# Scores of all 16 heads in one unit: four row strips and four PSUM banks at once, in place of two units of two strips

## The reference, cut to what matters

```python
# "gqa" (layer 0): 16 query heads, 4 key heads, width 32
scores = jnp.einsum('btkgd,bskd->bkgts', qg, k) * scale
scores = scores + mask[None, None, None]
p = jax.nn.softmax(scores, axis=-1)
out = jnp.einsum('bkgts,bskd->btkgd', p, v).reshape(B, T, C)
return out @ wo.T + bo
# "decay" (layer 1, self): no softmax
scores = jnp.einsum('bhid,bhjd->bhij', qb, kb) * intra_decay[None]
# "causal" (layer 1, cross): 16 heads, width 32
scores = jnp.einsum('bhqd,bhkd->bhqk', qh, kh) * inv_sqrt_d
scores = jnp.where(causal, scores, jnp.finfo(scores.dtype).min)
attn = jax.nn.softmax(scores, axis=-1)
```

## Time and profile before

| | |
|---|---|
| median of 3 runs | 2109.41 us (2105.24 to 2112.19) |
| the profiled execution | 2104.9 us, its span 2104.9 us |
| TensorE matmul busy | 1932.6 us, 92% |
| TensorE weight loads busy | 1575.4 us, 75% (they overlap the matmuls) |
| VectorE busy | 1044.6 us, 50% |
| ScalarE busy | 711.8 us, 34% |
| GpSimd busy | 386.6 us, 18% |
| mean granted TensorE clock | 0.969 |

### The profile page before, as it was taken

How to read it: one execution, slowest core, us unless ns; L and a number is a source line. 1 busy time by engine, 2 the same in 40 slices (tenths; PEclk the granted TensorE clock), 3 DMA queues, 4 the chain that set the end, 5 groups by cost and what they waited for, 6 DMA issues and landing times. The chain is left out here.

```text
span 2104.9 us, 32789 instructions
## 1 busy us (share of the span) xinstructions
PE 1932.6 (92%) x12124; PEld 1575.4 (75%) x12124; DVE 1044.6 (50%) x1836; ACT 711.8 (34%) x2275; POOL 386.6 (18%) x339
## 2 busy tenths in 40 slices
PE   8999888999999979999899999899979996999991
PEld 6777677788888757877678877677758874899990
DVE  5676753455555455333455556676755232222224
ACT  4555634344444422212221112444632211233332
POOL 2110100000000056000021100000104222644335
PEclk9999999999999989999999999999999998999995
DMA  7211051000000021000290001000015100644257
GB/s 236 59 42 42 1 193 47 1 1 1 1 1 1 1 106 60 0 0 0 92 388 6 1 31 41 1 1 1 2 46 185 66 0 0 240 136 154 80 112 204
DMA packets 73376, 135.89 MB, mean 65 GB/s; under 512 B 13457, under 2 KB 31761, under 8 KB 71185
## 3 DMA queue, kind: packets, MB, share of 16 engines
q1 hardware_dynamic: 47376, 96.28, 13.2%
q0 software_dynamic: 7888, 27.94, 4.5%
q10 hardware_dynamic: 17968, 9.71, 1.8%
HBM read 90.62 MB, written 43.29 MB: 64 GB/s over the span
## 5 line engine op out<-in xcount | busy, mean ns | idle before, releaser
L1470 PE MATMUL banks<-ternary_xth,ternary_wq 128*128 (+1 forms) x352 | 141.0, 401 | 5.3 <-DVE ternary_wq L1401 3.9
L1470 PE MATMUL banks<-ternary_xtl,ternary_wq 128*128 (+1 forms) x352 | 139.4, 396 | 0.0
L571 ACT ACTIVATE causal_pr<-banks,causal_nb 128x128 f32<-128x128 f32 x256 | 89.9, 381 | 52.3 <-DVE causal_nb L713 52.3
L97 PE MATMUL banks<-latent_vh,latent_cth 128*128 128x512 f32 x256 | 104.2, 407 | 3.5 <-DVE latent_ctl L1171 3.5
L97 PE MATMUL banks<-weights,expert_xgh 128*128 x312 | 104.8, 336 | 2.4 <-DVE expert_xgl L2083 2.4
L571 ACT ACTIVATE gqa_pr<-banks,gqa_nb 128x128 f32<-128x128 f32 x256 | 89.9, 382 | 45.5 <-DVE gqa_nb L713 45.5
L99 PE MATMUL banks<-weights,expert_xgl 128*128 x312 | 101.5, 325 | 0.0
L98 PE MATMUL banks<-weights,expert_xgh 128*128 x312 | 101.5, 325 | 0.0
L99 PE MATMUL banks<-latent_vh,latent_ctl 128*128 128x512 f32 x256 | 100.2, 391 | 0.0
L98 PE MATMUL banks<-latent_vl,latent_cth 128*128 128x512 f32 x256 | 100.1, 391 | 0.0
L1430 DVE TENSOR_TENSOR ternary_hf<-ternary_sg,banks 128x512 f32<-128x512 f32 x44 | 30.2, 687 | 135.5 <-issue 79.6
(11 more groups left out here) (462 smaller groups left out, 5538.4 us busy)
## 6 DMA issues: line engine op xcount, KB each, us to landing
x_slots<-decay_zeros SPq DMA_DIRECT2D x39, 256.0 KB, 4.6
y_slots<-decay_zeros SPq DMA_DIRECT2D x39, 256.0 KB, 4.9
y_slots<-expert_ys SPq DMA_DIRECT2D x39, 256.0 KB, 2.1
expert_xin<-x_slots SPq DMA_DIRECT2D x38, 256.0 KB, 2.9
weights_raw<-in_expert_experts SPq DMA_DIRECT2D x4, 2176.0 KB, 9.7
gqa_tw<-in_ternary_w ACTq DMA_DIRECT2D x4, 2112.0 KB, 10.7
ternary_raw<-in_ternary_w SPq DMA_DIRECT2D x11, 768.0 KB, 4.1
expert_raw<-in_expert_experts POOLq DMA_DIRECT2D x3, 2176.0 KB, 10.0
```

What stands on the lines that cost most here:

```text
L97: pe.matmul(out, wh, xh, start=first, stop=False, **kw)
L571: a = act.activation(pr[:, h, c, :], S.bank[2 * h + c // 4][:, (c % 4) * P:(c % 4 + 1) * P], ACT.Exp, bias=nb[:, h, c:c + 1], accum_out=su ...
L1470: a = pe.matmul(dst[:, :], wq[:, j, m, c * P:(c + 1) * P], x[:, c, toks], start=c == 0 and n == 0, stop=c == C - 1 and n == 1)
```

## The change

TensorE makes the scores of a batch in slot 0 for all four strips, and does nothing for the entry `S` in slot 1. It waits once for both halves of the batch before, and signals `s_full` once for a batch. VectorE's and ScalarE's work and order stay: the second half's maximum and exponentials keep their places in slot 1.

```diff
-                sp.wait_ge(s_full, 2 * (B - GT))
+                sp.wait_ge(s_full, B - GT)
...
                 elif what == "S" and soft:
-                    dve.wait_ge(s_full, u + 1)
+                    dve.wait_ge(s_full, b + 1)
...
                 elif what == "S":
-                    dve.wait_ge(s_full, u + 1)
+                    dve.wait_ge(s_full, b + 1)
...
                 elif what == "S":
+                    if h == 1:
+                        continue
...
-                    if u >= 2:
-                        pe.wait_ge(exp_done if soft else pt_done, u - 1)
+                    if b >= 1:
+                        pe.wait_ge(exp_done if soft else pt_done, u)
                     if soft:
-                        for x in range(2):
-                            pe.matmul(S.bank[2 * h + x], identr[:, :], maskr[:, :].unsqueeze(1).broadcast_to((P, 4, P)),
+                        for r in range(4):
+                            pe.matmul(S.bank[r], identr[:, :], maskr[:, :].unsqueeze(1).broadcast_to((P, 4, P)),
                                       start=True, stop=False)
                     for j in range(4):
-                        for x in range(2):
-                            r = 2 * h + x
+                        for r in range(4):
                             rows = slice(D * r, D * r + D)
```

## The result

| | before | after |
|---|---|---|
| median of the runs | 2110.78 us (2105.24 to 2112.19, 4 runs) | 2125.77 us (2124.63 to 2129.51, 4 runs) |
| ratio, 95% interval | | 1.0085 (1.0069 to 1.0102) |
| span of the profiled execution | 2104.9 us | 2122.8 us |
| TensorE matmul busy | 1932.6 us | 1894.5 us |
| mean granted TensorE clock | 0.969 | 0.962 |

The changed kernel is slower by 0.85%, while the matmuls of the busiest engine are busy 38 us less. (The two medians alone give 0.71%, which lies inside the interval.) Most of the 17.9 us of span comes from the three attention phases. The lengths are read between instructions of the trace: the soft phases from the first mask product to the end of the last exponential, decay from the first score unit to that of batch 15, so without the last batch.

What follows compares the result with a forecast made beforehand. The prediction took a closed loop over TensorE, VectorE and ScalarE to bound the soft batches, and TensorE most of decay. Gqa +12.9, causal +8.5, decay -12.5 and low clock +13 gave +22 us: 2131 us, range 2113 to 2157.

Steps and rivals of the forecast that it cites:

- TensorE's own work: Merged soft score unit: 2.23 us in place of 3.5, 1.3 us less for each of 32 soft batches.
- The loop: Soft phases: unit through all engines to the next unit, 15.16 us against 15.17 now; without projections 13.58 against 10.79.
- The batches: Soft batches: gqa 2 to 10 gain nothing, except batch 4 +1.1; batch 11 +2.4; 12 to 14 +2.8 each; gqa +12.9 us.
- Causal's middle: Causal batches 2 to 10: pieces under 0.5 us each with both signs, taken as +1 us.
- Its start: Start of causal: batch 1's half-clock second unit of 3.15 us goes, the unit before grows some 0.4; -2.8 us.
- Decay: Decay phase: one of two 1.09 us units goes, won in 11 batches by 1.07 and the last by 0.7; -12.5 us.
- The low clock: Long TensorE stops before batches 12 to 15 and last transposes, both soft phases: 8 half-clock stretches of 1.7 us, +13 us.
- The sum: Whole kernel: 12.9+8.5-12.5+13 = +22 us, from the median 2109.41 to 2131 us.
- The exponentials stay hidden: Rival: second-half exponentials end by 13.9 us after the unit's start, TensorE stays the bound; 2056 us; chance 0.08.
- Only two strips at a time: Rival: only two strips run at once, unit 0.9 us longer, 10 us of decay's gain gone; 2170 us; chance 0.08.
- The clock stays low through the last batches: Rival: low clock persists through the last batches, +37 us in place of +13; 2155 us; chance 0.10.
- No low stretches: Rival: no half-clock stretches and the small pieces fall well; 2109 to 2115 us; chance 0.08.

Runs made afterwards that it cites:

- the added products' kernel: Changed kernel plus 15 unread mask products ahead of the unit's wait in batches 12 to 15 of gqa and causal; 2117.74 us, ratio 1.0056 to before.
- the fourth experiment: Changed kernel with the unit's score instructions issued two strips at a time, strips 0 and 1, then 2 and 3; 2157.39 us, ratio 1.0250 to before.
- The fifth experiment: Changed kernel with the second half's maximum and exponentials moved into slot 0, ahead of the output add, in soft phases; 2083.63 us, ratio 0.9891 to before.

## Why the prediction was right

It said 2131 us and slower; 2125.77 was measured, inside the range. The mechanism, a closed loop that grows as long as the old batch or longer, is what the trace shows; the close match of the low clock's total is in part luck. Step by step:

**TensorE's own work: right.** 2.23 us was forecast for the unit, 2.23 measured. The 32 score instructions take 1.10 us from first to the next line's, in place of 1.09 for 16. In the records the four strips start 7 ns apart and a round comes every 112 ns. At 128 columns four row strips are as good as four column strips in this trace (1.10 us beside the 1.08 of pv). The 0.27 us more, an estimate worked out from the Trainium skill ("TensorE: Matmul & The Clock Gate", section on measured speedup, whose figure is for 512 columns), is not there.

**The loop: right in kind, 0.17 us too long.** The terms, forecast and measured in batch 6: unit 2.23 and 2.23; projection and T 3.66 and 3.65; output product to its add 3.04 and 3.04; add to maximum 2.00 and **1.86**; maximum to exponentials 1.26 and 1.25; exponentials 2.90 and 2.90; semaphore 0.07 and 0.06. Sum 15.16 and 14.99. The one term that was mis-sized had a wait of the old kernel in it: there the maximum at 129.12 had to stand until the second unit's scores, started at 127.92 and 1.16 us long, were done at 129.08. Before, and then after, the last statistics instruction:

```profile
127.92 1.16 PE L864 MATMUL banks<-gqa_kt,gqa_qt 32*128 32x128 f32 x16
...
128.91 0.15 DVE L219 TENSOR_SCALAR gqa_ve<-gqa_mv 128x1 f32<-128x1 f32 x1
```

```profile
133.47 0.15 DVE L219 TENSOR_SCALAR gqa_ve<-gqa_mv 128x1 f32<-128x1 f32 x1
```

From the start of that instruction to the maximum it is 129.12-128.91 = 0.21 us before and 133.54-133.47 = 0.07 after. The same two values, within 0.01 us, stand in every soft batch where the maximum follows the statistics, and before it always starts 0.05 us behind the end of the scores. The change takes that unit away, and the term shrinks by 0.14. The same term is in the loop of the last batches: forecast 13.58, measured 13.41 in the one without low clock (batch 12 of gqa). About 1 us of waiting was forecast ahead of the masks; 0.42 us stands there and 0.34 at the bank wait behind rt, which the forecast didn't name and which costs nothing here, since the loop sets the period either way.

**The batches.** Batch 4 was forecast +1.1, measured +1.12; batch 11 +2.4, measured +2.29 (gqa), and +1.4, measured +1.3 (causal); batches 0 and 1 of gqa cancel, and do within 0.2 us in the runs without a low stretch there. With the low clock taken out, gqa is +11.0 for the forecast +12.9, almost all of the difference by the mis-sized term. Causal's middle came to +0.1 for +1. Its start gave -4.6 for -2.8: in the kernel before the clock stays at 0.50 from the stop of 2.63 us ahead of 1325.44 on until about 1334; in the kernel after the same stop, ahead of 1331.26, is followed by 0.50 until 1333 and a mean of 0.71 from there to 1335. Here a low stretch became shorter, which the forecast did not count.

**Decay: right within half a microsecond.** Eleven batches gave 1.12 to 1.2 us each, 12.4 in all, where 11 x 1.07 = 11.8 was forecast. The last batch, which the table leaves out, gave 0.55 (from its first unit to the transposes ahead of causal 19.75 us for 20.30) where 0.7 was forecast: 13.0 together for 12.5. Batches 0, 4, 8 and 12 gave nothing. In 0, 4 and 8 the time goes into the wait for xgl as forecast (1.32 us in batch 4, for 0.24); in 12 there is a new wait of 0.63 us for otl ahead of the output product, which the forecast did not name. The new unit there, beside the earlier trace rows:

```profile
1161.45 1.17 PE L867 MATMUL banks<-pair_qt,pair_kt 32*128 32x128 f32 x32
1162.56 0.50 PE L97 MATMUL banks<-pair_xgh,pair_wqh 128*128 128x512 f32 x1
```

1.11 us for all 16 heads, what 8 took.

**The low clock: right in size, with some luck.** Eight stretches of 1.7 us were forecast on the loop, 13 us. Seven of them came, 1.84, 1.18 and 1.47 us in gqa's batches 13 to 15, 1.48, 1.84, 1.07 and 1.60 in causal's 12 to 15 (each the period less 13.41, in batch 15 the last exponential less the 13.35 of batch 12): 10.5 us. Two more came where none was forecast: batch 3 of gqa (16.73 us where the experiment with one unit in the soft phases alone has 15.11) and batch 1 (15.14 where the added products' kernel has 13.54). The latter stands behind this stop, clock 0.50 after it:

```profile
53.42 0.63 PE L879 MATMUL banks<-ident,gqa_spread 128*128 128x128 f32 x4 [2.24 <-POOL gqa_spread L478]
```

```profile
55.00:57.00 2.00, 2.00 (x6) 1.57 (x5) 0.00 (x0) 2.00 (x14) 0.00 (x0) 0.50 0.00 0
```

In all 13.7 us. The trace of after has eight stops of 3.79 to 3.80 us, ahead of batches 13, 14 and 15 and of the last transposes in both phases, and each is followed by a stretch at 0.50. The one ahead of batch 12 of gqa, 2.89 us, is not; that of causal, 1.35 us, is. So seven of the eight forecast places were right, at 1.5 us each on average for 1.7; that makes 2.8 us less than forecast, and the two stretches in batches 1 and 3, which nobody forecast, added 3.2. The near match of 13.7 and 13 is that luck. Nor is the price a fixed one: behind the same stops of 3.80 us it was 3.15 us in the fourth experiment. The Trainium skill, "TensorE: Matmul & The Clock Gate", section on HAM oscillation, describes a kernel whose waits bring the clock down once in every turn of its loop and advises to restructure so that TensorE stays busy; the added products show the first half (no stop, clock 1.00), the moved maximum the second.

**The sum.** Forecast 12.9+8.5-12.5+13 = 21.9; measured 11.0 and 5.0 in the soft phases without the low clock, -12.4, 13.7, together 17.3, and 0.6 elsewhere, the last batch of decay included. The largest miss is causal, 5.0 for 8.5, about half of it at its start, where the low stretch became shorter.

**The rivals.** *The exponentials stay hidden*: no, they ended at 14.94 us after the unit's start and TensorE waited. The fifth experiment adds that this rival was priced too high: with the exponentials hidden at 9.3 us a batch takes 14.51 us, not 13.9, for a bank wait that the second unit used to cover. *Only two strips at a time*: no, by the unit's length; and forced into pairs it costs 0.5 us, not 0.9. *The clock stays low through the last batches*: no, the clock was 1.00 again from 232 to 234 in batch 13. *No low stretches*: no, the two soft phases have twelve.

## What to carry to other kernels

Merging two small units of the busiest engine also merges their waits: before counting the saved work, write down the closed loop from the merged unit through every engine back to it, and compare that sum with the period, in each kind of batch; where the saved engine is also the slowest (decay) the saving is real, and where the sum exceeds it the time goes up. Then look whether the consumers' order can be changed so that what frees the banks comes early: the merge that lost 0.85% wins 1.1% with one entry of the order moved (ratio 0.9891), and 1.3 to 1.4% with a further move or two, though that step is within the noise; 0.57% of that is decay's, and the rest needs both the merge and the move. A term of a loop taken from the old trace may hold a wait that the change removes; look at what stands directly ahead of each instruction.

## What the runs showed of the hardware that I had not expected

- Instructions of different row strips overlap even when they are issued as groups one after the other: strips 2 and 3 started beside the last rounds of strips 0 and 1, and the pair order cost 0.55 us a unit where two groups one after the other would have cost 1.1 (twice the 1.09 us of 16 instructions, less 1.10).
- The same stop of 2.24 us, ahead of the same instruction, was followed by a stretch at 0.50 in the kernel after (53.42) and by none in the kernel with added products, whose line is below and whose batch is 1.6 us shorter. Stops of this length can't be priced one by one; neither can 2.89 us (no low stretch) and 1.35 us (one), while all eight of 3.8 us in the kernel after were followed by one. Nor has a stretch one length: behind such a stop the clock was back at 1.00 by 232 in batch 13 of the kernel after, some 6 us on, and in the pair order still at 0.50 some 7 us on (240.00:242.00).

```profile
53.60 0.63 PE L886 MATMUL banks<-ident,gqa_spread 128*128 128x128 f32 x4 [2.24 <-POOL gqa_spread L479]
```
